# Three layers on one core: the gram of h in four column tiles of 32 tokens, three passes in the first FFN, and another order in the recurrent layer

## The reference

```python
x = x + 0.5 * ffn(layernorm(x), w_up, w_down)
x = x + attn(layernorm(x), Wf, Wi, Wh)
x = x + 0.5 * ffn(layernorm(x), w_up, w_down)

def ternary_linear(x, w):
    alpha = mean(abs(w))
    w_t = sign(w) * (abs(w) > 0.5 * alpha)
    rms = sqrt(sum(x * x, -1)) / sqrt(x.shape[-1])
    return einsum('bsd,fd->bsf', x / (rms + 1e-8), w_t)

def ffn(x, w_up, w_down):                 # 128 -> 512 -> 128
    return ternary_linear(gelu(ternary_linear(x, w_up)), w_down)

# attn, per feature, along the 256 tokens of a sequence:
# h[t] = sigmoid(x Wf) * h[t-1] + sigmoid(x Wi) * g(x Wh),  h[0] = 0.5
# g(z) = z + 0.5 if z >= 0 else sigmoid(z)
```

## Time and profile before

| | |
|---|---|
| median of 3 runs | 303.44 us (302.75 to 303.98) |
| the profiled execution | 303.66 us, of which the span 301.8 us |
| granted TensorE clock, mean | 0.989 |
| PE busy | 246.6 us (82%), 3757 matmuls |
| DVE busy | 254.3 us (84%) |
| ACT busy | 223.7 us (74%) |
| POOL busy | 219.5 us (73%) |

### The profile page before, as it was taken

One profiled execution on the slowest core, in us unless ns is written; L12 is line 12 of the kernel. 1 busy time (PEld: TensorE's weight loads), 2 busy tenths in 40 slices (PEclk: granted clock), 3 DMA queues, 4 the chain that ended last, 5 costly groups with the idle time before them and its releaser, 6 DMA issues.

```text
span 301.8 us, 9838 instructions
## 1 busy us (share of the span) xinstructions
PE 246.6 (82%) x3757; PEld 168.2 (56%) x3757; DVE 254.3 (84%) x798; ACT 223.7 (74%) x546; POOL 219.5 (73%) x390
## 2 busy tenths in 40 slices
PE   0559998899989998878778775749989899999974
PEld 0337676667766776344434432327667667767753
DVE  3768999999999998787789936679999988887883
ACT  1266998798879998677776763457988789989971
POOL 5889697797887766676766777894978879776231
PEclk9999999999999999999999999798999999999999
DMA  5970000000000000000000000000111211111122
GB/s 169 297 187 3 2 3 2 3 2 4 2 3 1 4 3 2 0 2 0 2 0 0 1 0 3 1 0 2 38 37 37 72 38 39 55 55 38 37 73 72
DMA packets 18047, 9.74 MB, mean 32 GB/s; under 512 B 592, under 2 KB 17872, under 8 KB 18000
## 3 DMA queue, kind: packets, MB, share of 16 engines
q1 hardware_dynamic: 16896, 8.39, 10.3%
q10 hardware_dynamic: 1104, 0.72, 0.8%
HBM read 4.92 MB, written 4.19 MB: 30 GB/s over the span
## 4 chain that ended last, share of the span: by engine, by line
DVE 32%; PE 26%; POOL 19%; issue 14%; ACT 6%; DMA 1%; POOLq 0%; DVEq 0%; ACTq 0%
DVE h_lo L570 10%; POOL root L194 8%; DVE X L590 7%; PE U L460 6%; DVE st L549 4%; PE U L405 4%; PE T L387 3%; PE U L406 3%; PE Y L460 3%; POOL xn L215 3%; DVE xt_lo L566 3%; PE G L432 3%; DVE h_half L578 2%; POOL inject L233 2%; ACT U L296 2%
## 5 line engine op out<-in xcount | busy, mean ns | idle before, releaser
L296 ACT ACTIVATE U<-U 128x1024 f32<-128x1024 f32 x64 | 65.7, 1026 | 29.9 <-PE U L406 29.9
L570 DVE SCALAR_TENSOR_TENSOR h_lo<-U,h_hi 128x1024 f16<-128x1024 f32 x64 | 77.9, 1217 | 1.6 <-ACT h_hi L302 1.6
L215 POOL TENSOR_SCALAR xn<-X,neg_mean,rstd 128x128 f32<-128x128 f32 x164 | 72.6, 455 | 4.0 <-DVE rstd L562 1.3
L405 PE MATMUL U<-xt_hi,up_w 128*128 128x512 f16 x128 | 50.9, 398 | 19.5 <-DVE h_lo L570 16.4
L302 ACT ACTIVATE h_hi<-U 128x1024 f16<-128x1024 f32 x64 | 65.9, 1030 | 1.0
L222 POOL TENSOR_TENSOR rms<-ssq,half 128x4 f32<-128x4 f32 x32 | 34.5, 1078 | 40.6 <-ACT square_junk L328 40.6
L445 PE MATMUL Y<-down_w,h_hi 128*128 128x128 f16 x512 | 60.9, 220 | 0.0
L445 PE MATMUL Y<-down_w,h_lo 128*128 128x128 f16 x512 | 60.6, 219 | 0.0
L406 PE MATMUL U<-xt_lo,up_w 128*128 128x512 f16 x128 | 50.5, 394 | 0.0
L445 PEld LDWEIGHTS Y<-down_w,h_lo 128*128 128x128 f16 x512 | 50.1, 98 | 0.0
L445 PEld LDWEIGHTS Y<-down_w,h_hi 128*128 128x128 f16 x512 | 49.3, 98 | 1.3
(11 more groups left out here) (71 smaller groups left out, 415.9 us busy)
## 6 DMA issues: line engine op xcount, KB each, us to landing
X<-in_L_attn_x SPq DMA_DIRECT2D x16, 256.0 KB, 5.1
out_x<-X SPq DMA_DIRECT2D x16, 256.0 KB, 2.3
up_raw<-in_L_ffn_w_up ACTq DMA_DIRECT2D x1, 256.0 KB, 3.9
down_raw<-in_L_ffn_w_down ACTq DMA_DIRECT2D x1, 256.0 KB, 4.9
gate_raw<-in_L_attn_Wh ACTq DMA_DIRECT2D x1, 64.0 KB, 4.4
gate_raw<-in_L_attn_Wi ACTq DMA_DIRECT2D x1, 64.0 KB, 4.1
gate_raw<-in_L_attn_Wf ACTq DMA_DIRECT2D x1, 64.0 KB, 4.1
```

What stands on the lines that cost most here:

```text
L215: m = eng.tensor_scalar(xn[:, n % 2, t, :], X[:, c, :], neg_mean[l][:, c:c + 1], rstd[l][:, c:c + 1], ALU.add, ALU.mult)
L296: eng.activation(U[part][:], U[part][:], ACT.Gelu, scale=1.0 / XN_SPLIT).then_inc(gelu_done, 1)
L405: pe.matmul(U[part][:, c, :], up_w[:, f0:f0 + P], xt_hi[:, F % 2, :], start=True, stop=False)
L570: vec.scalar_tensor_tensor(out=h_lo[:, F % 2, 2 * part:2 * part + 2, :], in0=U[part][:], scalar=H_SPLIT, in1=h_hi[:, F % 2, 2 * part:2 * p ...
```

## The change

`gram` works with four column tiles of 32 tokens and 32 columns. In the first FFN it sums three products, hi.T hi, hi.T lo and lo.T hi, which give the whole diagonal, so h_half is not made there, and rms_step has another factor; the second FFN keeps h_half and its two products. On VectorE the additions of an older group stand behind the first h_lo and no longer ahead of it. In the recurrent layer ScalarE writes its two xn tiles one after each of the first two sigmoids. For the last norm VectorE does the three small operations (`last_moments`), not POOL. At the layer's end the cast of the second FFN's first group, its low_part and its first up projection come earlier. The diff at its core, out of the order of the file where that reads better:

```diff
@@ gram (TensorE), COLS = 4, SIDE = 32, off_diag [P, TILES, SIDE]
-                pe.wait_ge(h_half_done, 2 * F + 2)
+                if F >= groups:
+                    pe.wait_ge(h_half_done, 2 * (F - groups) + 2)
...
-                for n in range(2):
-                    pe.matmul(G[n * HALF:(n + 1) * HALF, :, 0:HALF], ident16[:, n * HALF:(n + 1) * HALF], off_diag[:],
-                              start=True, stop=False, tile_position=(0, n * HALF))
+                for n in range(COLS):
+                    pe.matmul(G[n * SIDE:(n + 1) * SIDE, :, 0:SIDE], ident16[:, n * SIDE:(n + 1) * SIDE], off_diag[:],
+                              start=True, stop=False, tile_position=(0, n * SIDE))
...
-                        for part in (h_half, h_lo):
-                            for n in range(2):
-                                i = slice(t * P + n * HALF, t * P + (n + 1) * HALF)
-                                m = pe.matmul(G[n * HALF:(n + 1) * HALF, t, 0:HALF], h_hi[:, par, c, i], part[:, par, c, i],
+                        for left, right in ((h_hi, h_hi), (h_hi, h_lo), (h_lo, h_hi)) if F < groups else ((h_hi, h_half), (h_hi, h_lo)):
+                            for n in range(COLS):
+                                i = slice(t * P + n * SIDE, t * P + (n + 1) * SIDE)
+                                m = pe.matmul(G[n * SIDE:(n + 1) * SIDE, t, 0:SIDE], left[:, par, c, i], right[:, par, c, i],
@@ h_halves (VectorE)
+                if F < groups:
+                    return
@@ the step of VectorE
+                if r == groups - 1:
+                    low_part(groups)
                 if 0 <= s - 24 < groups:
                     stats(2, s - 24)
                     mean_var(2, s - 24)
+                    i = link_of(2, s - 24)
+                    if sum(links(2)[i][1:]) == s - 24 + 1:
+                        last_moments(i, *links(2)[i][1:])
                 if in_ffn:
                     if F + 1 not in (groups, 2 * groups):
                         low_part(F + 1)
-                    finish_ffn(k, q)
                     h_low(F, 0)
                     h_halves(F, 0)
-                if in_ffn:
+                    finish_ffn(k, q)
                     h_low(F, 1)
                     h_halves(F, 1)
...
-                if r == groups - 1:
-                    low_part(groups)
@@ last_moments (VectorE, new)
+                dve.wait_ge(mv_done[2], i + 1)
+                vec.tensor_scalar(var_eps[2][:, i, 0:w], var, s * RMS_EPS ** 2, LN_EPS * s * RMS_EPS ** 2,
+                                  ALU.mult, ALU.add).then_inc(var_set[2], 1)
+                vec.tensor_scalar(var_eps[2][:, i, w:2 * w], var, s, None, ALU.mult).then_inc(var_set[2], 1)
+                vec.tensor_scalar(neg_mean[2][:, cols(first, w)], mean, -1.0, None, ALU.mult).then_inc(var_set[2], 1)
@@ the recurrent step of ScalarE
-                if r + 1 < groups:
-                    turned(groups + r + 1)
-                for n in range(3):
-                    gate(r, n)
+                turned(groups + r + 1)
+                gate(r, 0)
+                if by_both(groups + r + 2):
+                    norm_tile(groups + r + 2, 2)
+                gate(r, 1)
+                if by_both(groups + r + 2):
+                    norm_tile(groups + r + 2, 3)
+                gate(r, 2)
                 if r == 0:
                     sum_squares(groups - 1)
-                if by_both(groups + r + 2):
-                    norm_rest(groups + r + 2)
...
             act.preload_act_table(ACT.Gelu)
-            turned(2 * groups)
@@ up, F == groups (TensorE)
-                    pe.wait_ge(scan_done, groups - 1)
+                    if part == 1:
+                        pe.wait_ge(scan_done, groups - 1)
```

More of the change, by code:

```diff
@@ L20 @@
 POOL_TILES = 2
-HALF = P // 2
+COLS = 4
+SIDE = P // COLS
 OFF_DIAGONAL = -float(2 ** 60)
@@ L68, in build_macaron @@
         rstd = [sb(f"rstd{l}", [P, tiles]) for l in range(3)]
-        var_eps = [sb(f"var_eps{l}", [P, 2, 4 * TILES]) for l in range(3)]
+        var_eps = [sb(f"var_eps{l}", [P, groups if l == 2 else 2, 4 * TILES]) for l in range(3)]
         root = [sb(f"root{l}", [P, 2, 4 * TILES]) for l in range(3)]
@@ L186, in ln_roots @@
                 var = mv[l][:, cols(first, w), 1]
[L187 to L192, removed]
+                if l == 0:
+                    pool.wait_ge(mv_done[l], i + 1)
+                    eng.tensor_scalar(var_eps[l][:, par, 0:w], var, s * RMS_EPS ** 2, LN_EPS * s * RMS_EPS ** 2,
+                                      ALU.mult, ALU.add).then_inc(var_set[l], 1)
+                    eng.tensor_scalar(var_eps[l][:, par, w:2 * w], var, s, 1.0, ALU.mult, ALU.mult).then_inc(var_set[l], 1)
+                    eng.tensor_scalar(neg_mean[l][:, cols(first, w)], mv[l][:, cols(first, w), 0], -1.0, 1.0,
+                                      ALU.mult, ALU.mult).then_inc(var_set[l], 1)
                 pool.wait_ge(var_set[l], 3 * (i + 1))
-                eng.tensor_tensor(root[l][:, par, 0:2 * w], var_eps[l][:, par, 0:2 * w], half[:, 0:2 * w],
+                eng.tensor_tensor(root[l][:, par, 0:2 * w], var_eps[l][:, i if l == 2 else par, 0:2 * w], half[:, 0:2 * w],
                                   ALU.pow).then_inc(root_done[l], 1)
@@ L223, in rms_step @@
                 pool.wait_ge(rms_ready, F + 1)
[L225 removed]
+                eng.tensor_scalar(rms_den[:, par, :], rms[:, par, :], 2.0 * ((1.0 if F < groups else 2.0) / dff) ** 0.5, 2.0 * H_SPLIT * RMS_EPS,
                                   ALU.mult, ALU.add).then_inc(rms_den_done, 1)
@@ L287, in norm_rest @@
                 act.wait_ge(xt_ready, n - 1)
[L288 to L292, removed]
+                c = g * TILES + t
+                eng.activation(xn[:, n % 2, t, :], X[:, c, :], ACT.Identity, bias=shift[:, c:c + 1],
+                               scale=rstd[1][:, c:c + 1]).then_inc(xn_act_ready, 1)
             def gelu(F, part):
@@ L428, in gram @@
                         last = t == TILES - 1 and c == chunks - 1
-                        for part in (h_half, h_lo):
-                            for n in range(2):
-                                i = slice(t * P + n * HALF, t * P + (n + 1) * HALF)
-                                m = pe.matmul(G[n * HALF:(n + 1) * HALF, t, 0:HALF], h_hi[:, par, c, i], part[:, par, c, i],
-                                              start=False, stop=last and part is h_lo, tile_position=(0, n * HALF))
+                        for left, right in ((h_hi, h_hi), (h_hi, h_lo), (h_lo, h_hi)) if F < groups else ((h_hi, h_half), (h_hi, h_lo)):
+                            for n in range(COLS):
+                                i = slice(t * P + n * SIDE, t * P + (n + 1) * SIDE)
+                                m = pe.matmul(G[n * SIDE:(n + 1) * SIDE, t, 0:SIDE], left[:, par, c, i], right[:, par, c, i],
+                                              start=False, stop=last and (left is h_lo if F < groups else right is h_lo), tile_position=(0, n * SIDE))
                 m.then_inc(gram_done, 1)
@@ L558, in mean_var, with last_moments @@
                     m.then_inc(mv_done[l], 1)
+            def last_moments(i, first, n):
+                w, s = n * TILES, XN_SPLIT ** -2
+                mean, var = mv[2][:, cols(first, w), 0], mv[2][:, cols(first, w), 1]
+                dve.wait_ge(mv_done[2], i + 1)
[3 more added lines that the diff above has]
+                vec.tensor_scalar(neg_mean[2][:, cols(first, w)], mean, -1.0, None, ALU.mult).then_inc(var_set[2], 1)
             def scales(i, l, first, n):
```

16 lines of the change are left out of this document (8 added, 8 removed).

## The result

The changed kernel takes 337.8 us (median of four, 333.8 to 339.7) against 303.6 before. The prediction said 295 us, and its range ended at 302. It was wrong in sign.

A forecast was written before the change was run, and what follows sets the result against it. VectorE was taken to bound the first FFN and half the second, waits and rings the rest. Terms -1.7 - 5.0 - 2.6 + 1.4 - 0.8 + 0.3 - 0.2 = -8.6 took 303.66 us to 295; range 290.5 to 302.

The forecast's parts named there:

- rival C: TensorE's instruction packets: a first-FFN gram waits about 0.5 us where none is two ahead, +7, 302 us; chance 0.07.
- First FFN, -1.7 forecast: First FFN: steps of 5.87 us against 5.98 over some 14 steps, -1.7 us, with TensorE nearly full.
- The set of four: First-FFN gram: four 32-column matmuls with loads, taken at 28 ns, between 23 and 31; gram 1.34 us, +0.34.
- VectorE's saved 0.67 us a step: First FFN: two h_half of 0.33 us each leave VectorE, so its pace goes from 5.94 to 5.27 us.
- Rival A: Grams of both FFNs: TensorE pays 15.7 ns per matmul whatever the columns, total 330 us; chance 0.13.
- holes inside the gram: Sign of the instruction-packet rival: holes in TensorE's gram about as long as an instruction packet.
- Recurrent stretch, -5.0 forecast: Ten recurrent steps: six of 3.8 us, three of 5.05, one of 4.0; 42.0 against 47.0 us, -5.0.
- Rival B: Recurrent stretch: inject waits for the second sigmoid, scan for inject; step stays 4.2 us, total 298 to 299; chance 0.15.
- End of the recurrent stretch, -2.6 forecast: Steps r = 12 to 15: three small POOL operations leave the ring, -0.65 us each, -2.6 in all.
- The ring: End of the recurrent stretch: the loop root, scan, candidate, inject, root, forecast at 5.4 us root to root, from 6.06.
- Second FFN, +1.4 - 0.8 + 0.3 - 0.2 forecast: First half +1.4 for last_moments, second half -0.8, open gram(15) +0.3, gram(31) at the end and narrower sums of squares -0.2.
- The -0.8: Second half of the second FFN: additions leave the ring, steps of about 5.78 against 5.88 us, -0.8 over eight.

The follow-up runs named there:

- x6: Changed kernel with two column tiles, and three passes without h_half in both FFNs instead of the first alone: 295.7 us.
- x7: Changed kernel with two column tiles, and the last norm's three small operations back on POOL: 295.1 us, 0.973 times the kernel before.
- the spread kernel: Changed kernel with each tile's 48 gram matmuls followed by its quarter of the down projection in the first FFN: 323.4 us, 1.062 times the kernel before.

## Why the prediction was wrong

**The step that failed** is rival C's price: "16 KB and 1.0 us each ... where a packet isn't two ahead it waits about 0.5 us a gram, +7: 302", and with it its chance of 0.07. The mechanism was named, with the right size of a packet (250 instructions worked out, 256 measured). Two things in its price were wrong, and the sum that gave 295 had no term for the supply at all. The packet's 1.0 us was the DMA's own time; from the entry into one packet to the first instruction of the next it is 3.45 to 4.0 us, of which the DMA is between a quarter and a third. And it was charged against a gram of 1.3 us alone, where the mean over the step decides: 480 instructions are 1.9 packets, at 3.7 us each 7.0 us. Worked out so, 7.0 - 5.98 is 1.0 us a step. Measured are 2.1 (8.12 - 5.98), since the fetches are seldom back to back and the clock falls besides. Against the two-tile kernel, which has the same products, the 13 steps take 28.4 us more (105.6 for 77.2): 20.8 are the 14 holes, and the four stretches at half clock cost at most 6.8. The kernel before uses 218 instructions a step of 5.98 us (2399 over eleven steps), far from a packet in 3.5 us, so no row of it could show the latency. The prediction put the transfer's duration in its place, as if that were a bound from above; it was one from below. An unbounded cost on an engine that is "nearly full" should have carried more than 0.07.

**First FFN, -1.7 forecast, +34.4 measured.** The set of four was taken at 28 ns (23 to 31) and measured 32. With two tiles, where next to nothing is starved, 13 steps take 77.2 us for 78.3 before, a gain of 1.1 us where 1.7 were forecast for 14. So VectorE's saved 0.67 us a step bought 0.09, since TensorE was full in its place (64.75 of 65.0 us). In that trace scan(1) still comes 1.2 us later than before, by its slower start. Of the +34.4 the supply has the other 33: 25.4 us are the 17 holes up to gram(15), and the five stretches at half clock, 17 us together, cost at most 8.5, so little else is needed.

**Rival A** gave 330 us, near the measured, by a price that isn't there: matmuls at 15.7 ns each would have filled the gram evenly. They ran at 8.0 and stopped. That this time came near was luck. A time that fits doesn't make its mechanism right; the sign that the prediction had set for C ("holes inside the gram") decided it, though their length is not a packet's 1.0 us but 0.3 to 2.6 us.

**Recurrent stretch, -5.0 forecast.** From scan(1) to scan(7) 21.9 us for 28.4 before, -6.5; r = 7 to 11 +0.7 (last_moments 0.37 us a step, 0.35 forecast; steps of 5.06, 5.05 forecast). From scan(1) to scan(11) that is -5.8. The forecast of 3.8 for the first six was 0.14 too high, and TensorE's and VectorE's 3.64 and 3.7 were both nearer. The ten steps of 4.70 were a mean, besides: one of them, scan(7) to scan(8), took 5.87 us, and it did gain (5.48, and 4.74 with ScalarE's order alone). Rival B, inject as the last thing before each scan at over 4.1, did not come: 3.66.

**End of the recurrent stretch, -2.6 forecast.** Measured -4.8 from scan(11) to scan(15). The ring was to be 5.4 and is 5.2, and the first of these steps, 8.67 before, is 6.44 (7.45 with ScalarE's order alone). That step wasn't in the sum; what of it is POOL's shorter queue wasn't tested apart.

**Second FFN, +1.4 - 0.8 + 0.3 - 0.2 forecast, +11.6 measured to the end.** Again the supply: ten of the 27 holes, 12.0 us. With two tiles it is +2.8. The -0.8 was for steps of 5.78 instead of 5.88; with two tiles the last eight come to alternate at a mean of 5.77 where they were 5.84 before, but the first of them takes 6.5, so that over the eight nothing is left of it. And the last group's way from its up projection to the end is 16.3 us for 14.5 (15.7 and 15.3 in x6 and x7, which have the same order), for which the sum had no term.

**With the supply out of the way** the sum comes close: 295 against the 296.4 of two tiles. But that is in part luck, since the recurrent layer's 3 us over the forecast cover three of the five that the FFNs fell short of it (2.9 and 2.1).

## What to carry to other kernels

Count TensorE's instructions, loads and matmuls both, over a step, divide by 256, and compare with 3.5 to 4 us a packet: a tiling that halves the tiles and doubles their number can be free on the array and still starve the engine. Pieces named "issue" in the middle of one loop, at another place each time, with a transfer of the instruction queue that ended 1.2 to 1.6 us before the engine goes on, are the sign of it. And a latency for which the profile has only the transfer's own duration has no upper bound yet: measure it with a run of short, independent instructions before an edit rests on it.

## What the runs showed of the hardware beyond that

- A packet's period under full demand was 4.00 us with matmuls of 32 columns and 3.45 us with 64, although the first leaves the engine idle for longer. The granted clock was 0.5 under nearly all of the first and 1.00 under the second, but in the changed kernel two transfers also start 3.7 to 4.0 us apart at a clock of 1.00 (from 134 to 154 us). What sets the period between 3.4 and 4.0 stays open.
- With their loads, a set of four matmuls of 32 columns took 32 ns and a pair of 64 columns 31 ns. At half clock the set still took 33 ns and the pair 53: the pair goes with the array's clock, the set doesn't. At full clock alone the two can't be told apart. So four tiles of 32 columns bring nothing over two of 64 there.
- The granted clock fell to 0.5 in nine stretches, 31 us together, in the changed kernel (two before), five of them in the first FFN; the spread kernel had none there with the same instructions. All five began 0.0 to 1.5 us behind a hole of 1.9 to 2.6 us (ends of the holes 31.1, 41.4, 86.0, 95.6 and 114.1; clock down at 32.2, 42.4, 86.8, 97.1 and 114.1), but the holes of 2.3 and 1.9 us that ended at 105.6 and 145.0 had none behind them. One of them, from the table of stretches:

```profile
98.00:100.00 2.00, 2.00 (x10) 0.98 (x8) 0.25 (x4) 0.00 (x0) 1.85 (x5) 0.50 0.00 0
```

That is the lower of the two levels, 1.2 GHz: ten matmuls fill 2.0 us with no idle time, so part of what a hole costs is paid behind it.
